# Two attention layers on one core: order of the first stacks and rows of maxima, later copies in DRAM, semaphores by even and odd batch

## What is computed

```python
x  = L0_attn_x                                   # (8, 512, 128)
xn = layernorm(x)
s  = attn0(xn)      # 16 heads of 8; weights alpha*sign(W); softmax(q k^T / sqrt(8)) v; projection
g  = silu(moe(xn))  # 8 experts of 256, the best 2 of each token weighted, and one shared expert
x  = x + s * g
xn = layernorm(x)
s  = attn1(xn)      # 16 heads, q and k of 16 features; causal scores 1 + z + z*z/2 with z = q.k/4
g  = silu(coupling(xn))                          # 3 cycles of two small gate networks and a twist
x  = x + s * g
```

## Time and profile before

| | us |
|---|---|
| median of three runs | 1166.01 |
| the three runs | 1171.62, 1164.8, 1166.01 |
| the profiled execution | 1170.74 |
| its span, first to last instruction | 1168.9 |

### The profile page before, as it was taken

One profiled execution on the slowest core, in us unless ns is written; L12 is line 12 of the kernel. 1 busy time (PEld: TensorE's weight loads), 2 busy tenths in 40 slices (PEclk: granted clock), 3 DMA queues, 4 the chain that ended last, 5 costly groups with the idle time before them and its releaser, 6 DMA issues. The chain is left out here.

```text
span 1168.9 us, 19121 instructions
## 1 busy us (share of the span) xinstructions
PE 1011.8 (87%) x6984; PEld 524.4 (45%) x6984; DVE 703.2 (60%) x1103; ACT 655.9 (56%) x1407; POOL 310.2 (27%) x312
## 2 busy tenths in 40 slices
PE   4839999999999999799998369997359999999996
PEld 3613444344444443688887212222113455445543
DVE  5548998979899993233346823336037556666433
ACT  2207787768778788233322235554148667776663
POOL 3201010334425000266630010000655335533000
PEclk9557999879999999899999569999579999999999
DMA  6591220404224000577744000000899897978500
GB/s 197 174 331 57 75 99 32 149 25 158 79 88 165 3 3 2 168 219 224 222 126 128 27 5 1 0 0 1 82 112 108 88 100 89 97 89 97 65 1 19
DMA packets 76319, 108.24 MB, mean 93 GB/s; under 512 B 11618, under 2 KB 56676, under 8 KB 73540
## 3 DMA queue, kind: packets, MB, share of 16 engines
q1 hardware_dynamic: 69940, 89.18, 38.0%
q0 software_dynamic: 6288, 17.86, 4.4%
HBM read 56.20 MB, written 33.57 MB: 77 GB/s over the span
## 5 line engine op out<-in xcount | busy, mean ns | idle before, releaser
L821 DVE TENSOR_REDUCE a_nmax<-quad 128x2 f32<-128x1024 f32 x256 | 302.9, 1220 | 49.6 <-PE quad L521 47.8
L701 ACT ACTIVATE a_probs<-bank 128x512 f32<-128x512 f32 x339 | 191.0, 599 | 60.2 <-PE bank L538 33.8
L1696 ACT ACTIVATE a_probs<-quad 128x256 f32<-128x256 f32 (+3 forms) x512 | 182.8, 464 | 67.0 <-PE quad L1599 66.4
L550 PE MATMUL av<-a_probs,a_va 128*32 128x256 f32 x2048 | 171.3, 408 | 0.9 <-ACT a_probs L701 0.6
L1753 DVE TENSOR_TENSOR a_probs<-a_probs,const 128x512 f32<-128x512 f32 x128 | 117.1, 919 | 82.9 <-ACT a_probs L1696 82.2
L521 PE MATMUL quad<-k_stack,q_stack 24*128 24x512 f32 x512 | 136.9, 533 | 12.1 <-DVE a_nmax L821 9.9
L538 PE MATMUL bank<-q_stack,k_stack 26*128 26x512 f32 x339 | 140.1, 518 | 0.3 <-DMA q_stack<-a_nparts 0.2
L701 ACT ACTIVATE a_probs<-misc 128x512 f32<-128x512 f32 x173 | 103.4, 598 | 57.1 <-PE bank L538 53.4
L1137 POOL DMA_INDIRECT expert_rows<-m_ob,m_xr x78 | 74.6, 957 | 151.8 <-DVE m_ob L1236 126.1
L1565 POOL TENSOR_TENSOR a_rest<-a_full,a_parts 128x512 f32<-128x512 f32 x32 | 41.8, 1308 | 274.4 <-DVE a_parts L1745 272.8
L1599 PE MATMUL quad<-q_stack,k_stack 96*128 96x256 bf16 (+3 forms) x512 | 106.3, 308 | 8.5 <-ACT a_probs L1696 3.1
(11 more groups left out here) (244 smaller groups left out, 1514.6 us busy)
## 6 DMA issues: line engine op xcount, KB each, us to landing
m_wu<-packed_weights SPq DMA_DIRECT2D x39, 384.0 KB, 3.6
spread<-a_parts SPq DMA_DIRECT2D x48, 256.0 KB
q_stack<-a_parts SPq DMA_DIRECT2D x96, 128.0 KB, 6.8
k_stack<-a_parts SPq DMA_DIRECT2D x96, 128.0 KB, 7.4
q_stack<-spread SPq DMA_DIRECT2D x8, 1024.0 KB, 5.9
k_stack<-spread SPq DMA_DIRECT2D x8, 1024.0 KB, 9.6
sorted_rows<-in_shape_constants POOLq DMA_DIRECT2D x1, 5200.0 KB, 23.1
m_xr<-sorted_rows SPq DMA_DIRECT2D x39, 130.0 KB, 2.9
```

The costliest lines, as they stand in the source:

```text
L550: last = pe.matmul(av[STRIP * j:STRIP * (j + 1), at], va[b % 2][:, kt, GH * j + c, :], probs[:, (GH * s + j) % 8, at], start=(kt == 0 and ...
L701: act.activation(probs[:, (GH * s + j) % 8, :], col_bank(n)[:, :], ACT.Exp, scale=scale).then_inc(col_free, 1)
L821: dve.tensor_reduce(nmax[quad % 2][:, at:at + 2 * TT:TT], row_slot(n)[:, :, :], AX_X, ALU.max, negate=True)\
L1696: act.activation(probs[:, (64 * b + n) % 12, kt * P:T], quad[:, n % 4, kt * P:T], ACT.Square, bias=1.0, scale=0.25)\
```

## The change

Four edits:

1. In SP's loop, with b = -1, the spreading of batch 1 moves from c = 0 to c = 2 (behind the rows of quad 0), and its stacking from c = 1 to c = 3 (behind the rows of quad 1). Other batches keep their order.
2. GpSimd issues the fill of `sorted_rows` behind the splits of batch 2 and the packing of the weights behind the splits of batch 3. Both were behind the splits of batch 1.
3. The five steps that binarise the weights count on one semaphore.
4. In the second attention each half has one semaphore for even and one for odd batches. SP's `stack` of batch b waits for the landing of the earlier batches of b's own parity, no longer for that of batch b-1. PE's and DVE's waits are rewritten for the new counts.

```diff
@@ attention0, SP
-                    if c == 0 and b + 2 < B:
+                    if c == (0 if b >= 0 else 2) and b + 2 < B:
                         spread(b + 2, 0)
                         spread(b + 2, 1)
-                    if c == 1 and b + 2 < B:
+                    if c == (1 if b >= 0 else 3) and b + 2 < B:
                         stack(b + 2)
@@ attention0, GpSimd
             split_one(1, 0, split_q)
             split_one(1, 1, split_k)
-            pads = ...
-            pool.dma_start(S["sorted"]...).then_inc(padded, 16)
-            for n, name in enumerate(("w_gate", "w_up")):
-                pool.dma_start(S["packed"]...).then_inc(packed, 16)
-            for k in range(CHUNKS):
-                pool.dma_start(S["packed"]...).then_inc(packed, 16)
+            def lay_pads():
+                pads = ...
+                pool.dma_start(S["sorted"]...).then_inc(padded, 16)
+
+            def pack_weights():
+                for n, name in enumerate(("w_gate", "w_up")):
+                    pool.dma_start(S["packed"]...).then_inc(packed, 16)
+                for k in range(CHUNKS):
+                    pool.dma_start(S["packed"]...).then_inc(packed, 16)
...
             for b in range(2, B):
                 split_one(b, 0, split_q)
                 split_one(b, 1, split_k)
+                if b == 2:
+                    lay_pads()
+                if b == 3:
+                    pack_weights()
                 if b == 4:
@@ attention0, TensorE
-            pe.wait_ge(multiplied, 1)
+            pe.wait_ge(binarised, 5)
@@ attention0, VectorE
-            dve.tensor_reduce(alpha[:, 0:4], w[:, :, :], ...).then_inc(summed, 1)
+            dve.tensor_reduce(alpha[:, 0:4], w[:, :, :], ...).then_inc(binarised, 1)
             dve.wait_ge(signed, 1)
-            dve.tensor_tensor(diff, sign, w, ALU.subtract).then_inc(differed, 1)
-            dve.wait_ge(summed, 1)
-            dve.tensor_scalar(alpha[:, 4:8], alpha[:, 0:4], ...).then_inc(meaned, 1)
-            dve.wait_ge(differed, 1)
-            dve.tensor_tensor(binary, w, diff, ALU.add).then_inc(rebuilt, 1)
-            dve.wait_ge(rebuilt, 1)
-            dve.wait_ge(meaned, 1)
-            dve.tensor_tensor(weights, binary, alpha[:, 4:8], ALU.mult).then_inc(multiplied, 1)
+            dve.tensor_tensor(diff, sign, w, ALU.subtract).then_inc(binarised, 1)
+            dve.wait_ge(binarised, 1)
+            dve.tensor_scalar(alpha[:, 4:8], alpha[:, 0:4], ...).then_inc(binarised, 1)
+            dve.wait_ge(binarised, 2)
+            dve.tensor_tensor(binary, w, diff, ALU.add).then_inc(binarised, 1)
+            dve.wait_ge(binarised, 4)
+            dve.tensor_tensor(weights, binary, alpha[:, 4:8], ALU.mult).then_inc(binarised, 1)
@@ attention1
-        stack_a, stack_b = sem("stack_a"), sem("stack_b")
+        stacked = [[sem(f"stacked{half}{par}") for par in range(2)] for half in range(2)]
@@ attention1, SP, stack(b, par, half)
-                done = stack_b if half else stack_a
-                wait(sp, done, STACK * b)
+                done = stacked[half][par]
+                wait(sp, done, STACK * (b // 2))
                 wait(sp, split, 4 * b + 2 + 2 * half)
                 wait(sp, s_mm, 64 * (b - 2) + 32 * (half + 1))
@@ attention1, TensorE, score(b, par, t, j)
-                    wait(pe, stack_a, STACK * (b + 1))
+                    wait(pe, stacked[0][par], STACK * (b // 2 + 1))
...
-                    wait(pe, stack_b, STACK * (b + 1))
+                    wait(pe, stacked[1][par], STACK * (b // 2 + 1))
@@ attention1, VectorE, cast(b, k)
-                wait(dve, stack_b if half else stack_a, STACK * b)
+                if b >= 1:
+                    wait(dve, stacked[half][(b - 1) % 2], STACK * ((b - 1) // 2 + 1))
                 dve.tensor_copy(parts[k][:, 0, :], full[op][:, :]).then_inc(qk_cast, 1)
```

More of the change, by code:

```diff
@@ L267, in attention0 @@
         loaded, loaded1, ident_in, small = sem("w_loaded"), sem("w1_loaded"), sem("ident_in"), sem("small_loaded")
-        signed, summed, meaned, differed = sem("signed"), sem("summed"), sem("meaned"), sem("differed")
-        rebuilt, multiplied, w_turned, w_copied = sem("rebuilt"), sem("multiplied"), sem("w_turned"), sem("w_copied")
+        signed, binarised = sem("signed"), sem("binarised")
+        w_turned, w_copied = sem("w_turned"), sem("w_copied")
         w1_turned, w1_copied = sem("w1_turned"), sem("w1_copied")
@@ L443, in _ @@
             split_one(1, 1, split_k)
-            pads = io["shape_constants"][:, CONST_COLS + PAIR_COLS:].rearrange("p (o n) -> p o n", o=1)
-            pool.dma_start(S["sorted"].rearrange("(m p n) c -> p m (n c)", p=P, n=PADS),
-                           pads.broadcast_to([P, ROOM * UNIT // (P * PADS), PADS * ROW])).then_inc(padded, 16)
-            for n, name in enumerate(("w_gate", "w_up")):
-                pool.dma_start(S["packed"][:, :, DFF * n:DFF * (n + 1)], io["L0_ffn_" + name]).then_inc(packed, 16)
-            for k in range(CHUNKS):
-                pool.dma_start(S["packed"][:, :, 2 * DFF + k * C:2 * DFF + (k + 1) * C],
-                               io["L0_ffn_w_down"][:, k * P:(k + 1) * P, :]).then_inc(packed, 16)
+            def lay_pads():
+                pads = io["shape_constants"][:, CONST_COLS + PAIR_COLS:].rearrange("p (o n) -> p o n", o=1)
+                pool.dma_start(S["sorted"].rearrange("(m p n) c -> p m (n c)", p=P, n=PADS),
+                               pads.broadcast_to([P, ROOM * UNIT // (P * PADS), PADS * ROW])).then_inc(padded, 16)
+            def pack_weights():
+                for n, name in enumerate(("w_gate", "w_up")):
+                    pool.dma_start(S["packed"][:, :, DFF * n:DFF * (n + 1)], io["L0_ffn_" + name]).then_inc(packed, 16)
+                for k in range(CHUNKS):
+                    pool.dma_start(S["packed"][:, :, 2 * DFF + k * C:2 * DFF + (k + 1) * C],
+                                   io["L0_ffn_w_down"][:, k * P:(k + 1) * P, :]).then_inc(packed, 16)
             def number_rows(k):
@@ L797, in _ @@
             dve.wait_ge(loaded, 16 * 4)
-            dve.tensor_reduce(alpha[:, 0:4], w[:, :, :], AX_X, ALU.add, apply_absolute_value=True).then_inc(summed, 1)
+            dve.tensor_reduce(alpha[:, 0:4], w[:, :, :], AX_X, ALU.add, apply_absolute_value=True).then_inc(binarised, 1)
             dve.wait_ge(signed, 1)
-            dve.tensor_tensor(diff[:, :, :], sign[:, :, :], w[:, :, :], ALU.subtract).then_inc(differed, 1)
-            dve.wait_ge(summed, 1)
-            dve.tensor_scalar(alpha[:, 4:8], alpha[:, 0:4], 1.0 / C, None, ALU.mult).then_inc(meaned, 1)
-            dve.wait_ge(differed, 1)
-            dve.tensor_tensor(binary[:, :, :], w[:, :, :], diff[:, :, :], ALU.add).then_inc(rebuilt, 1)
-            dve.wait_ge(rebuilt, 1)
-            dve.wait_ge(meaned, 1)
+            dve.tensor_tensor(diff[:, :, :], sign[:, :, :], w[:, :, :], ALU.subtract).then_inc(binarised, 1)
+            dve.wait_ge(binarised, 1)
+            dve.tensor_scalar(alpha[:, 4:8], alpha[:, 0:4], 1.0 / C, None, ALU.mult).then_inc(binarised, 1)
+            dve.wait_ge(binarised, 2)
+            dve.tensor_tensor(binary[:, :, :], w[:, :, :], diff[:, :, :], ALU.add).then_inc(binarised, 1)
+            dve.wait_ge(binarised, 4)
             dve.tensor_tensor(weights[:, :, :], binary[:, :, :], alpha[:, 4:8, None].broadcast_to([P, 4, C]), ALU.mult)\
-               .then_inc(multiplied, 1)
+               .then_inc(binarised, 1)
             normalise(0)
```

## The result

| | before | changed |
|---|---|---|
| median, us | 1165.89 (1161.09 to 1171.87, 18 runs) | 1170.4 (1167.82 to 1178.56, 18 runs) |
| the profiled execution, us | 1170.74 | 1168.76 |
| its span, us | 1168.9 | 1166.6 |

The ratio of changed to before is 1.0048, with a 95% interval of 1.0027 to 1.0069: some 5.6 us slower, less than the 1% bound of the chances. The prediction was 1161.7 us, with a range of 1151 to 1170, so both missed: the sign, and the range by 0.4 us. So the traces are compared stage by stage, not by their ends.

The account below looks back on a forecast made before the run. TensorE, busy nearly all the main loop, pays its gaps in full: 1170.74 - 15.0 + 5.0 + 5.4 + 0.3 = 1166.4 us profiled. The 4.3 us saving, applied to the 1166.0 median, gave 1161.7 us, range 1151 to 1170.

Parts of the forecast that it names:

- the 1% bound of the chances: Whole kernel: a measurement tells about 1%, 11.7 us, from no change; chance 0.71 of landing within it.
- the sum: Whole kernel: 1170.74 - 15.0 + 5.0 + 5.4 + 0.3 = 1166.4 us for the profiled execution, 4.3 us less.
- The same here is 113.57 + 13.4 = 126.9 us: Before step 12: batch 2's spread lands 13.4 us after its last issue, making the step 5.0 us late.
- The check against the bandwidth: Fill plus batch 2's spread: clearing both at 343 GB/s takes 20 us, until about 129, so 126.9 fits.
- The clock: Behind the gap before step 12: TensorE at half speed until step 17's gather, costing 5.4 us, bounds 0 and 7.
- The upper bound of 6 us: Packing beside batch 3's spread: the most it costs, should it make a gap that takes the clock with it.
- would be in at 171.8: Rows of quad 7, issued 165.53 to 170.52: landed at 171.8, wanted at 172.64; the packing's cost taken as 0.3 us.
- Edits 3 and 4: Weight binarising: nothing, or up to 0.1 us gained; second attention: 0, since the lost wait was never last.
- Rival 2: Quad 3's rows wait for the whole fill, 10.7 us; packing holds quad 7's rows too, 6 us; 1173 us, chance 0.14.
- The sign that was to decide: Before step 12: a gap over 9 us would mean the rows of quad 3 wait for the fill's end.
- Rival 1: Before step 12: spread and fill share engines evenly, quad 3's rows land in time; 1151 us, chance 0.24.
- Rivals 3 and 4: Second attention landing waits fall away, 1147 us, chance 0.03; batch 1's stacks late for step 8, 1156 us, chance 0.05.

Follow-up runs that it names:

- the repeat: The changed kernel run once more, unchanged, on the third chip: 1174.51 us, ratio 1.0052 to the kernel before.
- The two runs above: Changed kernel with the fill made twice, first into a spare tensor: 1272.24 us; changed kernel with the fill waiting for batch 2's spread to land: 1254.01 us.
- the fastest kernel: Changed kernel with the fill after batch 0's stacks land, packing behind batch 1's splits: 1239.43 us, ratio 0.9871 (second chip); 1154.61 us, 0.9896 (third).

## Why the prediction was wrong

**Edit 1, right for the whole, wrong as a part.** 15.0 us were forecast and 15.25 were won (13.9 in the repeat). SP's rows came at 62.20 (forecast 62.6), the first score at 68.43 (68.8), the stacks of batch 1 at 77.53 (79), and step 8 had no gap. But the sum gave the whole gain to the order of the queue. Alone, this order wins 10.3 us, since its rows land late beside the copies, and edit 2 alone wins as good as all of it. In the sum of the whole change this did no harm: edit 2 was costed at its new place only.

**Edit 2, the step that failed: "The same here is 113.57 + 13.4 = 126.9 us".** It carried the landing of batch 1's spread over to batch 2's by its distance from the last issue. In the kernel before, that spread had a head start. It was issued from 49.32, and the fill was put in only by 51.14 + 1.08 = 52.22. One stretch of before, which the prediction did not read, shows what was moved by then. Behind it stands the same stretch in the DMA view (packets, MB, share of 16 engines), where SP's queue q1 is the only one with traffic:

```profile
48.00:52.00 4.00, 1.72 (x13) 1.16 (x11) 1.35 (x2) 3.26 (x5) 3.89 (x4) 0.92 0.36 136
```

```profile
q1 hardware_dynamic: 292, 0.54, 36.4%
```

That is 0.54 MB of the spread's 1.57 MB. The other 1.03 MB took the 14.4 us at full engines, from 52 to 66.4 us: 72 GB/s. In the changed kernel the fill is issued at 93.12, before the spread at 93.35, so all 1.57 MB go at about this rate: 22 us, and 22.9 were measured (69 GB/s). Counted as the prediction did, from the last issue at 97.67, the spread landed after 18.6 us and not 13.4. That puts the rows of quad 3 in at 115.78 instead of 112.0, in new time, and the gap is 8.94 us instead of 5.0. The check against the bandwidth ("126.9 is in the middle of what the bandwidth allows") gave false comfort. It said when both transfers together can be over, about 129, and the measured landing is 116.28 + 15.25 = 131.5 in old time, behind that end.

**The clock: right.** 5.4 us were forecast for the half-speed stretch behind the gap. The fill cost 13.6, less the gap of 8.9: 4.7 us. Of these, 0.9 fall in step 12 (forecast 1.1), 3.5 up to the turn after step 16 (3.7) and 0.3 behind it (0.6).

**The packing: the second error, a term mis-sized.** 0.3 us were forecast and 5.4 measured. The rows of quad 7 were to be in 1.2 us after their last issue, 0.8 us ahead of need. SP issued them until 163.91 + 4.99 = 168.90, and the score that waited for them starts at 172.75: 3.8 us. The gap of 1.65 us is this delay less what was spare, and the rest of the 5.4 is clock. The upper bound of 6 us, "should it make a gap that takes the clock with it", was the right case. The step that failed is "would be in at 171.8": it gave the rows the 1.2 us of a quiet queue. The prediction's own sum had the engines at work until about 172, with the spread of batch 3 ahead of these rows in SP's queue. So it was: from 158 to 170 us the engines move 371 GB/s, SP's queue has 1.51 MB of it, and the stacks that wait for the spread go at 172.58, 12.45 us after its last issue. How much of the 3.8 us is the spread ahead and how much the packing beside, no run here separates.

**Edits 3 and 4: right.** The kernel with them alone is no other than before (0.9983). VectorE's wait in the second attention is as it was; DVE's timeline of the changed kernel beside the earlier trace rows:

```profile
840.80 0.76 DVE L1752 CAST a_parts<-a_full 128x512 bf16<-128x512 f32 x2 [15.12 <-DMA k_stack<-a_parts]
```

With edits 3 and 4 alone the same wait is 15.18 us.

**The sum with the measured terms.** -15.25 + 8.9 + 4.7 + 5.4 = +3.8 us in place of -4.3. On a median near 1166 this makes 1170, and 1170.4 was measured. Taking the difference to the median of before, and not to its profiled execution, was right: that execution holds a stretch at half clock which others don't.

**The rivals.** Rival 2 is what happened, in its mechanism: both copies hold up rows in front of a score, and the clock goes with both gaps. Its size, 1173 us, came from the rows waiting for the fill to its end (10.7 us, counted from the end of the fill's issue, while the view counts the 23.1 us from its start: 9.6). In the changed kernel they do come in with the fill's end, 115.78 beside 115.8 us. The sign that was to decide, a gap over 9 us, can't: it is 8.94 us in one execution and 9.07 in the other. The two runs above decide. With the fill doubled the rows land at 127.8 us, 11.6 us ahead of the fills' end. Issued behind the landed spread they take 6.2 us and are in at 111.80, with the fill over at 102.08 + 23.8 = 125.9. Rival 1, an even share of bytes, is excluded: the spread got a sixth of them while the fill was on its way. The rule of the Trainium skill ("DMA: Bandwidth & Descriptors", section "Queues, rings and completion order") was right nevertheless: its turns are by packet, and the trace agrees, with 497 packets of SP's queue to 522 of GpSimd's. Shares of bytes follow from it only with the sizes of the packets, here 1.8 and 8.3 KB. Rivals 3 and 4 did not show.

## What to carry to other kernels

A transfer's landing measured beside another one must not be carried over as a delay: take the bytes that were still to move when the other began, divide by the time, and use that rate with the new start. The DMA view of that stretch gives packets and bytes by queue, and beside a copy with other packets the rate is another one: the same spread got a sixth of the bytes beside the fill and a third beside the packing. Before moving a bulk copy away from one wait, look at what it will meet: 5.3 MB cost nothing that can be told in a stretch where no engine waits for a transfer (the first score at 69.72 us, with 70.48 in the changed kernel on the same chip), and 13.6 us issued together with 1.6 MB that stands in front of a few KB on the critical path. And where two edits aim at one wait, run each alone before adding their gains; here one of them held the entire gain and also the entire loss.

## What was not expected of the hardware

**Small transfers beside busy DMA engines.** Eight rows of a few KB are in at most 1.1 to 1.2 us after their last issue on quiet engines. Beside GpSimd's DRAM copies it is 3.3 us (fill, at 68 us), 5.4 (both copies) and 6.2 (fill, at 106 us), and 11.1 us with the slowed spread in front. Why the first three differ stays open.

**Half clock on a busy TensorE.** It stays at 0.50 through stretches of 12.00 of 12.00 and 16.00 of 16.00 busy us (120 to 132, 176 to 192), on matmuls of 24 and 26 rows in the main. It stays so until 140 us, and then it is back at once, behind step 17, which brings the 128-row matmuls of the `gather`:

```profile
140.00:144.00 4.00, 3.85 (x40) 2.02 (x44) 3.39 (x6) 2.06 (x4) 0.00 (x0) 1.00 0.00 1
```

TensorE is no busier there than before. No run here had other rows at these places, so that they are the reason is not shown.

**One chip slower than the others.** On the second chip the kernel before takes 1255.56 us, against 1165.8 to 1168.5 on the other two, and every kernel with it. Waits appear there that the trace can't name, such as this one in the fastest kernel's timeline of ACT:

```profile
228.88 0.60 ACT L707 ACTIVATE a_probs<-bank 128x512 f32<-128x512 f32 x1 [9.96 <-remote]
```

ACT has 48.9 us of them in front of such instructions, in 8 places, from 228 us on, in the stretch in which GpSimd issues its indirect DMAs (206 to 411 us). Of that chip, only ratios to before on the same chip and events ahead of these waits are used above.
